# A new order of work at the slot boundary of a merged MLP and recurrence loop, on four engines

## What is computed

```python
x = x + mlp_out                                   # end of the first layer
xa = _ln(x, ln1_w, ln1_b)
sx = concatenate([state[:, 1:2] - xa[:, :1], xa[:, :-1] - xa[:, 1:]], axis=1)
xxx = tanh((xa + sx * maa_x) @ maa_w1).reshape(b, l, 5, DM)
xm = xa[:, :, None] + sx[:, :, None] * (maa_stack + einsum(xxx, maa_w2))
xk, xw, xv, xr, xg = (xm[:, :, j] for j in range(5))
w = exp(-exp(time_decay + tanh(xw @ td_w1) @ td_w2))
r, k, v = xr @ Wr.T, xk @ Wk.T, xv @ Wv.T ; g = silu(xg @ Wg.T)
out_t = r_t . (u * k_t v_t + s) ; s = k_t v_t + w_t * s      # scan over the 64 tokens
og = group_norm(out) * gn_w + gn_b
x1 = x + og * g @ Wo.T
# then channel mixing: x1 + sigmoid(xr2 @ Wfr.T) * (square(relu(xk2 @ Wfk.T)) @ Wfv.T)
```

## Time and profile before

| | |
|---|---|
| median of 3 runs | 1178.59 us (1177.57 to 1181.72) |
| profiled execution | 1175.96 us, span 1174.2 us |
| mean granted TensorE clock | 0.971 |
| busy share of the span | PE 93%, PEld 77%, DVE 77%, ACT 60%, POOL 50% |
| chain that ended last | PE 47%, issue 30%, POOL 12%, DVE 7%, ACT 3% |

### The profile page before, as it was taken

One profiled execution on the slowest core, in us unless ns is written; L12 is line 12 of the kernel. 1 busy time (PEld: TensorE's weight loads), 2 busy tenths in 40 slices (PEclk: granted clock), 3 DMA queues, 4 the chain that ended last, 5 costly groups with the idle time before them and its releaser, 6 DMA issues.

```text
span 1174.2 us, 34409 instructions
## 1 busy us (share of the span) xinstructions
PE 1091.8 (93%) x12992; PEld 906.4 (77%) x12992; DVE 906.2 (77%) x1677; ACT 706.3 (60%) x1606; POOL 592.9 (50%) x520
## 2 busy tenths in 40 slices
PE   5999999999999989999999999999999998887898
PEld 5889898888988977777778777777777776665587
DVE  5987778897777772277888978888788887898864
ACT  5778787777877764644555545554455535434475
POOL 4777877878788760243344443443334343332221
PEclk9999999999999989999999999999999999889999
DMA  9400000011111100033333123321333123304001
GB/s 334 144 4 1 0 0 3 21 39 48 38 45 36 45 11 1 15 73 75 82 81 71 25 68 81 80 55 30 76 80 80 26 55 82 81 1 117 19 36 54
DMA packets 39867, 65.01 MB, mean 55 GB/s; under 512 B 4384, under 2 KB 26208, under 8 KB 39392
## 3 DMA queue, kind: packets, MB, share of 16 engines
q1 hardware_dynamic: 39776, 63.75, 20.5%
HBM read 55.35 MB, written 8.39 MB: 54 GB/s over the span
## 4 chain that ended last, share of the span: by engine, by line
PE 47%; issue 30%; POOL 12%; DVE 7%; ACT 3%; DMA 0%; POOLq 0%; SPq 0%; DVEq 0%; ACTq 0%
PE psum L353 9%; PE psum L267 5%; PE psum L336 5%; PE psum L368 4%; POOL late_xm L892 4%; PE psum L297 3%; PE psum L280 3%; PE psum L982 3%; POOL shared L901 2%; POOL x L868 2%; PE psum L310 2%; PE psum L1250 2%; PE psum L1280 2%; PE psum L991 1%; DVE shared L1762 1%
## 5 line engine op out<-in xcount | busy, mean ns | idle before, releaser
L1762 DVE TENSOR_TENSOR_SCAN shared<-late_wT,shared 128x512 f32<-128x512 f32 x128 | 171.5, 1340 | 0.0
L892 POOL TENSOR_TENSOR late_xm<-late_mixed,late_xa 128x512 f32<-128x512 f32 x64 | 90.4, 1422 | 104.9 <-DVE late_mixed L1728 104.1
L232 POOL TENSOR_TENSOR shared<-shared,att_row_max 128x512 f32<-128x512 f32 x128 | 132.5, 1053 | 16.9 <-DVE att_row_max L564 16.9
L353 PE MATMUL psum<-shared 128*128 128x128 f32 x1024 | 127.3, 278 | 0.0
L1748 DVE TENSOR_TENSOR shared<-shared,psum 128x504 f32<-128x504 f32 x128 | 84.7, 672 | 52.9 <-ACT shared L1411 52.9
L353 PEld LDWEIGHTS psum<-shared 128*128 128x128 f32 x1024 | 121.5, 195 | 0.3 <-ACT shared L462 0.2
L453 ACT ACTIVATE shared<-shared 128x512 f32<-128x512 f32 x128 | 80.5, 631 | 68.3 <-POOL shared L232 68.2
L982 PE MATMUL psum<-late_glnT,w 128*128 128x256 f32 x512 | 119.5, 387 | 1.8 <-ACT late_glnT L1358 1.8
L991 PE MATMUL psum<-w,late_hT 128*128 128x256 f32 x512 | 118.6, 380 | 1.0 <-ACT late_hT L1367 0.9
L901 POOL TENSOR_TENSOR shared<-shared,late_rT 128x512 f32<-128x512 f32 x32 | 40.8, 1274 | 154.6 <-DVE shared L1762 154.6
L564 DVE TENSOR_REDUCE att_row_max<-shared 128x8 f32<-128x512 f32 x128 | 86.8, 680 | 41.0 <-POOL shared L225 41.0
(11 more groups left out here) (167 smaller groups left out, 2458.8 us busy)
## 6 DMA issues: line engine op xcount, KB each, us to landing
shared<-v_rows SPq DMA_DIRECT2D x64, 512.0 KB, 7.5
shared<-in_enc SPq DMA_DIRECT2D x64, 128.0 KB, 2.6
v_rows<-shared SPq DMA_DIRECT2D x64, 64.0 KB, 1.8
out<-x SPq DMA_DIRECT2D x16, 256.0 KB, 2.0
x<-in_x SPq DMA_DIRECT2D x7, 512.0 KB, 10.1
w<-in_w SPq DMA_DIRECT2D x2, 1024.0 KB, 17.2
shared<-in_cross_mask SPq DMA_DIRECT2D x1, 1024.0 KB, 12.0
shared<-in_w_qkv SPq DMA_DIRECT2D x1, 768.0 KB, 4.8
```

The costliest lines, as they stand in the source:

```text
L232: nc.gpsimd.tensor_tensor(zs, zs, peak.unsqueeze(2).to_broadcast([P, PAIRS, S]), ALU.subtract).then_inc(shifted, 1)
L353: last = nc.tensor.matmul(dst[:, half * P:(half + 1) * P], w[:, kb, c0 + half * P:c0 + (half + 1) * P], src[:, u % 2, kb, 0:P], start=(kb ...
L892: nc.gpsimd.tensor_tensor(xm[m % XM].rearrange("p h (b t) -> p (h b) t", t=S), mixed[:, m % 2, :, :].rearrange("p h (b t) -> p (h b) t", t=S),
L1762: nc.vector.tensor_tensor_scan(states, wT[:, u, half, :, :, :].rearrange("p j b t -> p (j b t)"), states, 0.0, ALU.mult, ALU.add).then_inc ...
```

## The change

Only the order of calls changes; no instruction is added or removed. TensorE: K of run s+1 goes ahead of `transpose(s+2)` and down part 3; behind R come `mlp_transpose` and `transpose_on`, then G; `bonus_sums`, head sums and `project_out` go ahead of `mixer`. POOL: `step_back` ahead of `make_bonus`. ScalarE: `mlp_copy_in` first, the mixer's tanh behind the states, the K copy ahead of `copy_in`, the R copy ahead of `copy_on`. VectorE: `mlp_residual` right behind the first product, `apply_gate` behind the first read and `mixer_input`, `gate` ahead of `add_bonus`, `mlp_moments` ahead of `add_residual`.

```diff
@@ gpsimd body
+                if there(s + 1):
+                    step_back(s + 1)
                 if there(s):
                     make_bonus(s, u)
-                if there(s + 1):
-                    step_back(s + 1)
@@ tensor body
+                if now:
+                    project(s, NR)
+                if mlp_run:
+                    mlp_transpose(s + 3)
                 if there(s - 2):
                     transpose_on(s - 2)
-                if now:
-                    project(s, NR)
-                    project(s, NG)
                 if early(s - 1):
                     ch_values(early_run(s - 1, 1), 1)
-                if mlp_run:
-                    mlp_transpose(s + 3)
-                if mixing:
-                    mixer(s + 1)
+                if now:
+                    project(s, NG)
                 if early(s):
                     ch_transpose(early_run(s, 0), 0)
                 if now:
                     bonus_sums(s)
-                if there(s - 2):
-                    project_out(s - 2)
                 if old:
                     sum_heads(s - 1, 2)
                     sum_heads(s - 1, 3)
+                if there(s - 2):
+                    project_out(s - 2)
+                if mixing:
+                    mixer(s + 1)
...
                 if mlp_run:
                     down(s + 3, 2)
+                if mixing:
+                    project(s + 1, NK)
                 if norm:
                     transpose(s + 2)
                 if early(s):
                     ch_receptances(early_run(s, 1), 1)
                 if mlp_run:
                     down(s + 3, 3)
-                if mixing:
-                    project(s + 1, NK)
@@ scalar body
+                if there(s + 3):
+                    mlp_copy_in(s + 3)
                 if there(s):
                     copy(s, u, NG)
...
-                if there(s + 3):
-                    mlp_copy_in(s + 3)
-                if there(s + 1):
-                    mixer(s + 1)
                 if early(s):
                     ch_copy_in(early_run(s, 0), 0)
                 if there(s - 1) and there(s):
                     set_states(s, 2)
                     set_states(s, 3)
+                if there(s + 1):
+                    mixer(s + 1)
...
+                if there(s + 1):
+                    copy(s + 1, 1 - u, NK)
                 if early(s):
                     ch_tanh(early_run(s, 1), 1)
                 if there(s + 2):
                     copy_in(s + 2)
                 if there(s + 1):
-                    copy(s + 1, 1 - u, NK)
+                    copy(s + 1, 1 - u, NR)
                 if there(s - 1) and not s_is(s, RUNS - 1):
                     copy_on(s - 1)
-                if there(s + 1):
-                    copy(s + 1, 1 - u, NR)
@@ vector body
                 if there(s):
                     key_values(s, 0)
+                if there(s + 2) and not s_is(s, -2):
+                    mlp_residual(s + 2)
...
-                    if n == 0 and there(s - 2):
-                        apply_gate(s - 2, u)
                     if there(s):
                         read(s, u, n)
                     if n == 0:
-                        if there(s + 2) and not s_is(s, -2):
-                            mlp_residual(s + 2)
                         if there(s + 1):
                             mixer_input(s + 1)
+                        if there(s - 2):
+                            apply_gate(s - 2, u)
...
+                    if n == 1 and there(s):
+                        gate(s, u)
                     if n == (1 if early(s) else 2) and there(s):
                         add_bonus(s, u)
-                    if n == 1 and early(s):
-                        add_residual(s - 2)
-                    if n == 1 and there(s):
-                        gate(s, u)
...
                     if n == 2:
-                        if there(s - 2) and not early(s):
-                            add_residual(s - 2)
+                        if early(s):
+                            ch_mix(early_run(s, 0), 0)
                         if there(s + 2) and not s_is(s, -2):
                             mlp_moments(s + 2)
-                        if early(s):
-                            ch_mix(early_run(s, 0), 0)
+                        if there(s - 2):
+                            add_residual(s - 2)
```

## The result

The changed kernel takes 1139.26 us (median of 4 runs, 1137.86 to 1139.99) against 1179.76 us for the kernel before in the same measurement (1177.57 to 1181.72): ratio 0.9665, 95% interval 0.9639 to 0.9690. The forecast was 1144. The profiled execution of after takes 1138.86 us (span 1137.1), 37.1 us less than that of before, with a mean granted clock of 0.988 instead of 0.971.

What follows compares the result with a forecast made beforehand. TensorE's own work plus its stops was taken as the bound. Terms summing to 33.9 off the profiled 1175.96 gave 1142.1; 2.6 for the timed median made 1144.7, stated as 1144, range 1132 to 1162 (8 in 10).

Steps and rivals of the forecast that it cites:

- up to the first product: Start of the kernel: the first K comes earlier, 2.2 us less.
- slots 0, 1: Stops of 2.2 and 1.9 us go, 0.25 a slot returns at `bonus_sums`; one clock fall in slot 1 goes; together 5.1.
- slots 2 to 12: Settled slots: eleven of 35.2 us instead of 407.15 us in all, 20.0 us less, about 11 of it the clock.
- slot 13: First slot with channel work: K and `bonus_sums` earlier win 8.2 us, 0.7 and about 1.0 come back; 6.6 less.
- slot 15 and tail: End of the kernel, taken together with slot 14: stops change places, zero gain, bounds 3 us either way.
- the new stop: TensorE at L1094, `bonus_sums` waiting for y: 1.05 us a settled slot, bounds 0.5 and 1.3.
- the slowing of `mixer_input`: VectorE at the slot boundary: `mixer_input` overlaps POOL's `make_bonus` by 0.72 us and loses 0.5 us.
- Rival (a): Slots 2 to 11: the clock still falls once in each, 1.6 us a slot, giving 1160; chance 13%.
- (b): Slot boundary: `apply_gate` or `mixer_input` another 1 us late each slot, 11 us less gain: 1155, or 1158; 12%.
- (c): Whole kernel: no change, from clock falls plus a replacement wait and late tail, or an order VectorE evens out; 4%.
- (d): First product: V's broadcast becomes the bound and the kernel slower, 1186 if landing 5 us late each slot; 4%.
- the step that costs `add_residual`: VectorE, `add_residual` behind `mlp_moments`: done about 1 us ahead of `mix_pair`, so free; without that cover some 0.7 us.

Runs made afterwards that it cites:

- e3: Changed kernel with four short VectorE statistics instructions, results unused, ahead of the product in `apply_gate`; 1172.01 us, ratio to before 0.9970.
- e11: Changed kernel with two short VectorE statistics instructions, results unused, ahead of the product in `apply_gate`; 1148.36 us, ratio to before 0.9780.
- e12: Changed kernel with three short VectorE statistics instructions, results unused, ahead of the product in `apply_gate`; 1154.19 us, ratio to before 0.9843.
- e5: Kernel before with only K moved ahead of the transposes on TensorE and its copy ahead of `copy_in` on ScalarE; 1160.51 us, ratio to before 0.9871.
- e4: Changed kernel with K's projection back behind the transposes and down part 3 on TensorE; 1162.21 us, ratio to before 0.9876.
- e7: Changed kernel with `make_bonus` back ahead of `step_back` on POOL; 1171.54 us, ratio to before 0.9949.
- e8: Changed kernel with `add_residual` ahead of `ch_mix` and `mlp_moments` on VectorE in slots 13 to 15 only; 1133.41 us, ratio to before 0.9643.
- e9: Changed kernel with `apply_gate` ahead of `mixer_input` on VectorE and `transpose_on` ahead of `mlp_transpose` on TensorE; 1127.95 us, ratio to before 0.9573.
- e6: Changed kernel with `mlp_residual` back behind the first read on VectorE; 1174.01 us, ratio to before 0.9979.

## Why the prediction was right, and where it wasn't

Measured by the starts of the first product of each run, profiled execution against profiled execution:

| step | forecast | measured |
|---|---|---|
| up to the first product | -2.2 | +1.0 |
| slots 0, 1 | -5.1 | -6.2 (68.17 to 61.94) |
| slots 2 to 12 | -20.0 | -24.1 (407.15 to 383.09) |
| slot 13 | -6.6 | -4.2 (46.68 to 42.48) |
| slot 14 | 0 | +0.2 (40.21 to 40.38) |
| slot 15 and tail | 0 | -3.8 (107.5 to 103.7) |
| sum | -33.9 | -37.1 |

**The boundary: right.** The chain was as worked out to 0.1 us up to `mixer_input`; the new stop came where it was said, for the releaser that was said, and e3, e11 and e12 show that a slot is 34.0 us and this stop (0.83, 1.48, 1.81, 2.14 give 34.80, 35.45, 35.79, 36.10). Of the signs named in advance one failed: slot 13 was to be under 41 us and took 42.48.

**Mis-sized: the slowing of `mixer_input`.** I took an overlap of 0.72 us with `make_bonus` and 0.5 us for it. `make_bonus` took 1.29 us instead of the 1.47 of the earlier trace rows, where it had started beside a scan (645.72 to 646.94 in the earlier trace rows), and `mixer_input` started 0.11 us later than worked out, so that the overlap was 0.43 us (641.90 to 642.33). It cost 0.22 us (1.10 against the 0.88 of the earlier trace rows). The same two instructions in slot 14, where they lay closer:

```profile
996.25 1.29 POOL L884 TENSOR_TENSOR shared<-late_rT,shared 128x512 f32<-128x512 f32 x1
996.60 1.63 DVE L1719 SCALAR_TENSOR_TENSOR late_xin<-late_sx,cols,late_xa 128x256 f32<-128x256 f32 x2
```

Of the 1.63 us the first of the two VectorE instructions took 1228 ns. It ended at 997.83, 0.29 us behind POOL's end at 997.54; at the settled boundary it took 708 ns and ended at 642.61, 0.28 us behind POOL's end. The four L1866 of the earlier trace rows show the same: the first ended 0.28 us behind POOL's 1041.24. So the VectorE instruction is held until the POOL instruction ends and is done 0.28 us later. Alone it takes 0.48 us, so the hold costs the overlap less 0.2 us: 0.23 for 0.43 here, and 0.52 for the 0.72 that I had assumed. The rule of the Trainium skill that the loser is blocked for the whole instruction ("SBUF — State Buffer", SBUF: two separate sides) agrees with this. The price for an overlap was right, and the overlap was mis-sized.

The stop came out at 0.83 for 1.05. From the start of `mixer_input` to that of the gate it was 1.03 us instead of 1.3, but the chain was 0.11 us late before it and 0.07 behind it, and TensorE was free at 8.38 instead of 8.24. TensorE's own work is 34.0 us for the 34.2 that I had as the difference of a slot and two stops; why it is less in the new order no run shows. Together this is 0.4 us a slot, the 4.1 us of slots 2 to 12.

**Slots 0 and 1.** TensorE has no stop at all in them: the 0.25 us a slot that I had `bonus_sums` pay for `make_bonus` isn't there, 0.5 of the 1.1 us more that they won.

**Rival (a), the clock: it didn't happen, and the margin wasn't thin.** I took 1.62 to 1.77 us of stops in before, after which it did and didn't fall, as a sign that 1.05 us stood near the edge. The runs put 0.83 and 1.5 us in a slot and nothing fell, so rival (a) deserved a few per cent rather than 13. The prediction also misread slot 4 of before: it had 1.77 us of stops, not 1.62. What decides near the edge isn't settled. In before the three slots with 1.62 us passed, and of the eight with 1.77 to 1.79 us seven fell; e5, with 1.58 to 1.62 us in two stops and as much work between them (0.66 us, before 0.63), passed everywhere, which fits. But the sum alone doesn't sort the slots: e4 with 1.84 to 1.91 us in two stops, 2.8 us of work apart, and e12 with 1.81 us in one kept the clock up in all eleven. And in before itself a slot without a fall and one with have all but the same stops, here slots 4 and 5:

```profile
648.77 0.66 PE L968 MATMUL psum<-ident,late_gxn 128*128 128x128 f32 x4 [1.21 <-DVE x L1696]
649.99 1.13 PE L1009 MATMUL psum<-late_xin,maa_w 128*128 128x256 f32 x4 [0.56 <-DVE late_xin L1718]
...
684.85 0.63 PE L968 MATMUL psum<-ident,late_gxn 128*128 128x128 f32 x4 [1.30 <-DVE x L1696]
685.97 1.57 PE L1009 MATMUL psum<-late_xin,maa_w 128*128 128x256 f32 x4 [0.49 <-DVE late_xin L1718]
```

The second pair is followed by slow matmuls (1.57 us for 1.13), the first isn't.

**Rivals (b), (c), (d): no.** In the settled slots TensorE has no wait beside the one at L1094. Rival (b) would have made the stop 1.05 + 1 = 2.05 us, which is that of e7, and so would have cost far more than the 11 us I gave it, since that stop brought the clock down in ten slots of eleven. The landing of V did hold the first product twice, for 1.62 us at the head of slot 3 and 0.90 us at that of slot 5. Counted between first products slot 2 so is 35.64 and slot 3 34.20, but TensorE's stop at L1094 is 0.82 us in slot 3 as in the others. VectorE's idle time ahead of `mlp_residual`, 0.78 us elsewhere, is gone in slot 3: it took the delay up, as the rival had it.

**Failed: the step that costs `add_residual` at "at most its own length, some 0.7 us".** In the slots with channel work the kernel before had `add_residual` a group earlier (`n == 1 and early(s)`); the diff takes that away, and I priced only the settled case. There it isn't `mlp_moments` alone that now stands ahead of it but also four L1867, 2.31 us. TensorE stood 4.46 us in slot 13 and 3.66 in slot 14, with the clock down behind each. The cover has to be counted again in each kind of slot; I counted it in the settled one. That is 2.4 us of slot 13: with the step undone in e8, slot 13 takes 40.05 us, the 6.6 us less that were forecast, and slot 14 wins 2.4 us more. (The terms of slot 13 as written, 8.2 - 0.7 - 1.0, give 6.5.)

**Slot 15 and tail.** VectorE's wait for `ch_values` (L1875 behind L1281) was 8.7 us in 4 before, 5.4 in 2 after, and TensorE's first stop in slot 15, 1.62 us at `transpose_on` for POOL's `scale` (L909), is gone, as R now stands ahead of it. New ones have come, 0.81 us at R and 1.11 us at head sums. Before also had the clock at its lower level for 6.8 us in slot 15, after not at all; e9, with such a fall and nearly the stops of after, takes 104.7 us for 103.7. No run takes these parts apart. 3.8 us is just over my bound of 3.

**The first product** should have come 2.2 us sooner and came 1.0 us later. By 448 us, with TensorE's work still the same in both, after was 3.2 us behind. Half of it, 1.6 us, is there at 430 us, ahead of the fall of the clock that both have, and I didn't look for its cause. In that fall the clock stood at its lower level for 10.2 us (from 434.7 to 445.0) where it stood for 6.8 before, and TensorE lost the other 1.6 us. K's share is real: e4, with K last, has its first product at 507.4, after at 505.5.

**The median.** Before had its median 2.6 us above the profiled execution, after 0.4. I carried the 2.6 over. The likely source is the clock, which falls in some slots in one run and in more in the next (before took 1168.5 to 1182.3 us over all measurements, at mean clocks of 0.981 to 0.967); the kernels whose clock stays up in the settled slots spread by 1.6 to 4.4 us, e12 apart (9.6). This made 2.2 of the 5.4 us by which the 1144.7 of the sum was too high, the steps 3.2.

## What to carry to other kernels

Follow the chain of release times over the boundary of a slot engine by engine; where its durations stand in the trace it comes out to a tenth of a microsecond, and the first thing that TensorE lacks then shows the next move (here the gate ahead of `mixer_input`, or the mixer, which doesn't need y, ahead of `bonus_sums`). Count the cover of a moved step again in each kind of slot, above all in those with extra work. And look at each stop of TensorE by itself, how long it is and what stands next to it, and not only at the total: from 1.8 to 2.14 us of stop a slot the kernel lost 17.8 us (e12 to e3), four times what thirteen slots of 0.33 us more come to.

## What the runs showed of the hardware

- One stop of TensorE a slot: 0.83, 1.5 and 1.8 us left the clock at 2.4 GHz in all eleven settled slots of the profiled execution, 2.0 to 2.2 us sent it to 1.2 GHz in 8 to 10 of eleven (e3, e6, e7). It holds for these slots only (2.56 us in slot 0 of e6 passed).
- Near the edge one execution differs from the next: e12 had mean clocks of 0.985 and 0.978 (1153.0 and 1162.6 us), before 0.981 and 0.971 (1168.5 and 1179.7 us).
- A slot with a fall takes 37.6 to 37.75 us nearly whatever the stop is (1.77 to 1.79 us in before, 2.0 to 2.1 in e6 and e7, 2.14 in e3; from `bonus_sums` to `bonus_sums`), whereas those without one differ: 35.84 in before, 36.1 in e3 and e7, 36.5 in e6.
- A VectorE instruction with two SBUF inputs that started while a POOL multiplication ran ended 0.28 to 0.29 us behind POOL's end, for overlaps of 0.40 to 0.95 us in after (0.48 us alone; 474 to 486 ns over 32 of them in e7, where there was no overlap). A VectorE multiplication with one input in PSUM (L1774, 641.30) wasn't slowed: 0.69 us, wholly beside the same POOL instruction.
